# Moving the norms, the logits and the choice of expert groups within the steps of a graph-attention and mixture-of-experts kernel

## The reference

```python
def layernorm(x): return (x - mean(x)) / sqrt(var(x) + 1e-5)
# graph attention
h = layernorm(x) @ W.T + b_W
e = (h @ a1)[:, None] + (h @ a2)[None, :] + b_a
e = where(e > 0, e, 0.2 * e)
x = x + softmax(where(adj > 0, e, -9e15), axis=1) @ h
# experts
xf = layernorm(x)
logits = xf @ Wr + br                       # 64 experts
gates = softmax(top_k(logits, 2))
x = x + sum over the two experts of gate * (relu(xf @ W1[e] + b1[e]) @ W2[e] + b2[e])
```

## Time and profile before

| what | value |
|---|---|
| median of 3 runs | 276.71 us (275.14 to 277.4) |
| profiled execution | 275.16 us, of which the span of the profile is 273.4 |
| granted PE clock, mean | 0.926 |
| PE / DVE / ACT / POOL busy | 227.0 / 208.4 / 180.2 / 167.0 us |
| start of DVE's step 8, 9 | 60.81, 74.11 |
| start of DVE's step 12, 13 | 90.90, 103.39 |
| start of DVE's step 14, 15 | 109.07, 120.67 |
| evac(15) of ACT starts | 135.32 |

### The profile page before, as it was taken

How to read it: one execution, slowest core, us unless ns; L and a number is a source line. 1 busy time by engine, 2 the same in 40 slices (tenths; PEclk the granted TensorE clock), 3 DMA queues, 4 the chain that set the end, 5 groups by cost and what they waited for, 6 DMA issues and landing times.

```text
span 273.4 us, 6241 instructions
## 1 busy us (share of the span) xinstructions
PE 227.0 (83%) x1863; PEld 215.0 (79%) x1863; DVE 208.4 (76%) x587; ACT 180.2 (66%) x425; POOL 167.0 (61%) x212
## 2 busy tenths in 40 slices
PE   1494899999699966978884749999999999999840
PEld 1354899999689966978773639999999999999740
DVE  6879999996999799699455505889886766676465
ACT  2748989999298947758334336887877777777300
POOL 5770003450899889778577753455888888866500
PEclk9999799999799999799995557999999999999995
DMA  6988665589429817108931122222168701100067
GB/s 155 210 161 152 129 119 79 159 228 236 120 66 284 229 39 272 41 10 320 418 120 39 51 63 66 71 66 63 46 185 295 246 31 38 35 31 22 31 198 273
DMA packets 11120, 36.89 MB, mean 135 GB/s; under 512 B 2256, under 2 KB 2832, under 8 KB 10320
## 3 DMA queue, kind: packets, MB, share of 16 engines
q0 software_dynamic: 5232, 14.98, 24.1%
q1 hardware_dynamic: 5424, 21.11, 22.6%
q10 hardware_dynamic: 432, 0.40, 0.7%
HBM read 39.36 MB, written 5.51 MB: 164 GB/s over the span
## 4 chain that ended last, share of the span: by engine, by line
PE 60%; DVE 15%; POOL 7%; DMA 7%; issue 5%; ACT 3%; SPq 1%; POOLq 0%; DVEq 0%; ACTq 0%
PE bank L1146 17%; PE bank L1158 16%; PE bank L1039 12%; PE bank L1015 8%; DVE arena L753 5%; POOL table L431 5%; DMA xs<-in_x 2%; DMA arena<-result 2%; PE bank L980 2%; PE bank L1135 2%; PE bank L1058 1%; PE bank L1055 1%; DMA rows_in<-table,arena 1%; DVE idx L773 1%; DVE hot L779 1%
## 5 line engine op out<-in xcount | busy, mean ns | idle before, releaser
L1039 PE MATMUL bank<-arena 128*128 128x130 f32 x512 | 61.5, 276 | 0.0
L1146 PE MATMUL bank<-arena 128*128 x384 | 60.9, 283 | 0.1
L1039 PEld LDWEIGHTS bank<-arena 128*128 128x128 f32 x512 | 59.5, 192 | 0.5 <-ACT arena L576 0.3
L1158 PE MATMUL bank<-w2s,arena 128*128 x384 | 59.2, 277 | 0.2 <-issue 0.2
L431 POOL DMA_INDIRECT table<-rows_in,pos x32 | 48.7, 1522 | 8.9 <-issue 8.5
L1146 PEld LDWEIGHTS bank<-arena 128*128 128x128 f32 x384 | 52.0, 197 | 0.6 <-issue 0.3
L1158 PEld LDWEIGHTS bank<-w2s,arena 128*128 128x128 f32 x384 | 51.0, 193 | 0.6 <-issue 0.6
L907 DVE SCALAR_TENSOR_TENSOR arena<-bank,arena 128x128 f32 x96 | 33.6, 350 | 22.3 <-PE bank L1158 21.0
L654 ACT ACTIVATE arena<-bank,arena 128x128 f32<-128x128 f32 x96 | 35.1, 366 | 19.0 <-PE bank L1146 17.7
L1015 PE MATMUL bank<-ident,arena 128*128 128x128 f32 x256 | 35.5, 299 | 12.9 <-DVE arena L753 12.9
L576 ACT ACTIVATE arena<-bank 128x512 f32<-128x512 f32 x64 | 34.0, 597 | 14.9 <-PE bank L1015 14.6
(11 more groups left out here) (195 smaller groups left out, 282.1 us busy)
## 6 DMA issues: line engine op xcount, KB each, us to landing
arena<-in_adj POOLq DMA_DIRECT2D x16, 512.0 KB, 6.6
w2s<-in_w SPq DMA_DIRECT2D x8, 768.0 KB, 4.5
arena<-in_w SPq DMA_DIRECT2D x6, 1024.0 KB, 9.3
arena<-in_w SPq DMA_DIRECT2D x4, 512.0 KB, 4.7
w2s<-in_w SPq DMA_DIRECT2D x4, 512.0 KB, 3.9
xs<-in_x SPq DMA_DIRECT2D x4, 256.0 KB, 6.5
arena<-result SPq DMA_DIRECT2D x2, 512.0 KB, 4.4
arena<-result SPq DMA_DIRECT2D x4, 256.0 KB, 5.9
```

The source lines that it names most:

```text
L1039: ins = pe.matmul(OB[t % 2][:, 0:D + 2], pt_r[:, t % 2, j, :], h[:, j, :], start=(j == 0), stop=(j == T - 1))
L1146: ins = pe.matmul(hp(p, b), w1u[:, p % UW, P * b:P * b + P], xT_all[:, bass.ds(column, P)], start=True, stop=True)
L1158: ins = pe.matmul(yp(p), hT[:, p % UH, b, :], w2s[:, bass.ds(u, 1), b, :].rearrange("p e d -> p (e d)"), start=(b == 0), stop=(b == HB - 1))
```

## The change

Groups 0 to 3 are early now. Norms of tiles s-4 and s-3 stand at the end of every even ACT step, behind `evac(s-1)`. PE transposes a group in the middle of `attend(LAST+2)`, ahead of its ninth product, makes the logits behind the products of that step, and counts behind `attend(LAST+3)`. ACT copies into `x2T` in step LAST+4 ahead of the evac. DVE chooses (`top2`) in step LAST+4 behind leaky, for groups 0 to 2; `place` stays in step LAST+5 behind leaky. On POOL the scatters of tiles 8 and 9 leave step 15: one tile's stand ahead of `rstd_of(6)`, the other's between it and `rstd_of(7)`.

```diff
-    PLACED = [(0, 0, 9), ..., (1, 7, 15), (2, 8, 15), (2, 9, 15)]
-    EARLY = 3
-    NORMED = [(5 + 2 * i, 2 * i) for i in range(5)]
+    PLACED = [(0, 0, 9), ..., (1, 7, 15)]
+    EARLY = 4
@@ POOL, behind the loop
+            place(2, 8)
             rstd_of(6)
+            place(2, 9)
             rstd_of(7)
@@ ACT
             def evac(t):
                 for b in range(4):
-                    for q in range(NG):
-                        if b == 2 and q < EARLY and t == LAST[q] + 3:
-                            route_a(q)
...
                 if s >= 3:
                     deviation(s - 3)
-                for at, t in NORMED:
-                    if s == at:
-                        norm(t)
-                        norm(t + 1)
                 for q in range(EARLY):
-                    if s == LAST[q] + 5:
-                        route_b(q)
-                if s == T - 1:
-                    route_a(3)
+                    if s == LAST[q] + 4:
+                        route_a(q)
                 if s >= 1:
                     evac(s - 1)
-                if s == T - 2:
-                    norm(T - 6)
-                    norm(T - 5)
+                if s >= 4 and s % 2 == 0:
+                    norm(s - 4)
+                    norm(s - 3)
+                for q in range(EARLY - 1):
+                    if s == LAST[q] + 4:
+                        route_b(q)
@@ DVE
                     residual(s - 3)
-                for q in range(EARLY):
-                    if s == LAST[q] + 5:
+                leaky(s - 1)
+                for q in range(EARLY - 1):
+                    if s == LAST[q] + 4:
                         top2(q)
-                leaky(s - 1)
-                for q in range(EARLY):
                     if s == LAST[q] + 5:
                         place(q)
@@ PE, attend(t)
-                for q in range(EARLY):
-                    if t == LAST[q] + 3:
-                        route_a(q)
-                if t == T - 2:
-                    route_b(3)
...
                     for q in range(EARLY):
-                        if j == T // 4 and t == LAST[q] + 3:
-                            route_b(q)
+                        if j == 8 and t == LAST[q] + 2:
+                            route_a(q)
...
                 ins.then_inc(s_o, 1)
+                for q in range(EARLY):
+                    if t == LAST[q] + 2:
+                        route_b(q)
@@ PE, the loop
-                for q in range(EARLY):
-                    if s == LAST[q] + 4:
-                        route_c(q)
                 turn(s)
                 attend(s)
-                if s == T - 3:
-                    route_a(3)
-                if s == T - 2:
-                    route_c(3)
+                for q in range(EARLY):
+                    if s == LAST[q] + 3:
+                        route_c(q)
```

More of the change, by code:

```diff
@@ L25, in build @@
     LAST = [START[q + 1] - 1 for q in range(NG)]
-    PLACED = [(0, 0, 9), (0, 1, 10), (0, 2, 11), (0, 3, 11), (1, 4, 13), (1, 5, 13), (1, 6, 13), (1, 7, 15), (2, 8, 15), (2, 9, 15)]
-    EARLY = 3
-    NORMED = [(5 + 2 * i, 2 * i) for i in range(5)]
+    PLACED = [(0, 0, 9), (0, 1, 10), (0, 2, 11), (0, 3, 11), (1, 4, 13), (1, 5, 13), (1, 6, 13), (1, 7, 15)]
+    EARLY = 4
     LNS = [(t, t + 2) for t in range(0, T - 2, 2)] + [(T - 2, T - 1), (T - 1, T)]
```

## The result

The changed kernel is slower: 288.38 us median of 4 runs (285.05 to 290.48) against 275.92 of the kernel before, ratio 1.045 (95% interval 1.029 to 1.061). Measured once more beside the experiments (e10), it came to 289.6, ratio 1.049 (1.042 to 1.055). Medians are over all executions of a kernel, while the ratios leave out those in a slower state, here the 290.48 and in e1 the 289.4. The profiled execution took 288.86 us, its span is 287.1, 13.7 us more than before. The profile before was of an execution of 275.16 us.

What follows compares the result with a forecast made beforehand. DVE was taken to set the pace of ordinary steps, ACT close behind. Terms +5.8, +4.8, -1.3, -1.6 and +0.5 gave +8.2 on 275.16, so 283.4, stated as 284.0 us; range 278 to 289.

Steps and rivals of the forecast that it cites:

- my own sum: Whole kernel: the terms for groups and tail add +8.2 us, forecast 284.0, own range 281 to 286.5, chance 0.60.
- the rival of the slower clock: PE behind its longer holes: lower clock adds +5.0 us over three groups, 288.4; chance 0.15.
- Group 0, +5.8: Loop up to DVE's step 9: norms waiting for POOL make logits late, step 9 starts at 79.9 against 74.11.
- The chain caught by leaky: POOL's chain for tiles 2 and 3: ends at 60.3 untouched, 62.9 if held by leaky; 62.8 taken.
- Group 1, +4.8: DVE's steps 9 to 13: POOL's late scale holds norms some 3 us; step 13 starts at 113.95, +4.8 more.
- Group 2, -1.3: DVE's steps 13 to 15: two-tile group with norms in time gains 1.3 us; step 15 starts at 129.95.
- The condition: Four-tile groups on DVE: break even only if logits (L') come 3.30 us sooner, since the next step's work follows top2.
- Tail, -1.6 and +0.5: After DVE's step 15 starts (D_15): evac(15) gains 1.6 us with ACT's r15 at +2.35; group 4's transposes cost 0.5.
- The sign that I named: Tail: ACT's 4.7 us wait for POOL gone, as one sign that the forecast is right.
- No wait for POOL, 276.6: Norms on ACT never wait for POOL, only their 0.98 us counts: +1.4 us, 276.6; chance 0.12.
- Scatters pass leaky: POOL's scatters run unheld beside leaky, so group 1 loses less: +5.2 us, 280.4; chance 0.08.
- Faster: ACT has caught up, so L560 of step l+4 (l: group's last tile) starts with DVE's scores: -3.3, 271.9; chance 0.05.

Runs made afterwards that it cites:

- e10: Changed kernel as it is, measured once more against the kernel before; 289.6 us, ratio 1.049.
- e1: Changed kernel with DVE's top2 back in step LAST+5 ahead of leaky, all else as changed; 285.6 us, ratio 1.037 to the kernel before.
- e6: Changed kernel with top2 back in step LAST+5 ahead of leaky and norms as plain copies not waiting for POOL; 270.92 us, ratio 0.985 to the kernel before.
- e2: Changed kernel with norm a plain copy that does not wait for POOL, scale and shift left out; 277.16 us, ratio 1.008 to the kernel before.
- E9: Changed kernel with unused extra transposes on PE ahead of its wait for norms in groups 0, 1 and 3; 286.19 us, ratio 1.039 to the kernel before.
- e8: Kernel before with ACT's norms alone moved to the end of even steps; 283.82 us, ratio 1.031.

## Why the prediction was right, and where its sum was short

I forecast 284.0 in a range of 278 to 289, slower with chance 0.85; it took 288.38, slower. The direction and the mechanism in the loop were right. The size was 4.4 us short, outside the 281 to 286.5 that I gave my own sum; only the room left for other cases holds it, and the second measurement, 289.6, lies above the range. That 288.38 is the figure of the rival of the slower clock is luck: the excess is of POOL and the clock together. Step by step:

- **Group 0, +5.8.** Measured +5.0 in the two profiles, +5.3 counted from step 0. ACT's first wait was 1.55 (1.6 forecast), L560's counterpart in step 7 came at 63.06 (63.8), the max at 68.39 (69.3). The chain caught by leaky is the term that I chose between bounds: 62.8, and it ended at 62.03. The nearest row, a chain caught in its first operation, was 0.8 us too dear; here two short operations slipped through and only the third was held. (The 1.44 that I gave an untouched chain was the wrong reading: it is how far the caught one ended behind leaky. Untouched it took 1.61, from 76.80 to 78.41. The sum goes by the caught one.) How close this is to chance the second profile of the same kernel, e10, shows, in step 4:
```profile
47.54 2.35 DVE L748 SCALAR_TENSOR_TENSOR arena<-arena,tneg 128x2048 f32<-128x2048 f32 x1
47.59 2.88 POOL L413 TENSOR_TENSOR rstd<-ve,expo 128x2 f32<-128x2 f32 x1
...
52.18 1.09 ACT L587 ACTIVATE rows_in<-xs,nm,rstd 128x256 f32<-128x256 f32 x2 [3.06 <-POOL nm L415]
...
81.72 2.28 DVE L742 CUSTOM_DVE_ANT_0 arena<-arena 128x2048 f32<-128x2048 bf16 x1
```
POOL's third operation began 0.05 us behind leaky here and was held, where in the first profile it began 0.25 ahead of it (46.89, 0.72 us long). ACT waited 3.06, not 1.55, and step 9 came 61.72 us behind step 0, not 58.79. The two executions took 291.67 and 288.86 us: group 0's loss is 5 us in one and 8 in the other.
- **Group 1, +4.8.** Measured +4.7 (33.95 against 29.28 us from step 9 to 13). But ACT waited 1.40 where I had 3: its own evac(9) had become late, behind a turn(8) of 3.10 us, so that the late scale and the slow clock lay side by side. The sum was right because the scale alone set it: L415 ended at D_9 + 16.9, as forecast.
- **Group 2, -1.3.** Measured -1.5.
- **The condition** (L' must come 3.3 us sooner) held: e1 shows 7.5 us from max to step 9 in the old order, the changed kernel 10.7, and e6 against e2 gives 6.2 us for the order in two such groups.
- **Tail, -1.6 and +0.5.** This is the step that failed. Evac(15) came 19.6 us behind the start of step 15, where I had 13.0 and before had 14.65: +4.9, not -1.6. I took r15 as D_15 + 2.35, that is, I let the norms of tiles 10 and 11 end in time. They ended 3.75 late, POOL's chain being held by scores and then by leaky behind scatters that had run to 128.18. The other 2.9 us are PE at its lower level, in the second half of attend(13) (3.67 us, not 1.96), the logits and turn(14); attend(14) took 3.75, the upper level's time. E9 bears this out: with the clock up the same distance was 16.64. The +0.5 behind evac(15) was right: spans differ by 13.7, evac(15) by 13.1. The sign that I named, ACT's wait for POOL in the tail gone, was half wrong: the one ahead of evac(15) fell from 4.73 to 1.58, and the new one of 3.75 stands ahead of step 15.
- **The rivals.** No wait for POOL, 276.6: e2 made that case, with norms 0.35 us a pair cheaper, and took 277.16. Slower clock, 288.4: I priced it as three turns on the path; where it can be counted it is about 3 us, in group 3, the place that I had named as without cover. Scatters pass leaky: they do not, L430 at 125.14 began as leaky ran (125.00) and took 3.04 us, as in the kernel before. Faster: nothing of it was seen in groups 0 and 1; step 7 of ACT came at 63.06, not below 58.

What stays open: in the tail POOL and clock are told apart by rows and by e9, but the wait for POOL also makes the holes behind which the clock falls, so that their shares of the whole loss can't be added up cleanly. Nor is it shown how much of e8's excess is the clock, nor why POOL's chain starts some tenths later in one execution than in another.

## What to carry to other kernels

When a small operation is moved earlier on an engine with an in-order queue, look up when its input is ready, and not only when its consumer wants it: norm pairs put ahead of 5 us of ScalarE's work let a chain of four tiny GpSimd operations set when the logits came. When a choice is moved from the middle of a step to its end, the work that used to cover the wait now stands behind it; the new input must come earlier by that work, or the move loses. And a part of a losing change can be a gain by itself: test the parts alone.

## What the runs showed of the hardware

GpSimd's tiny operations (128 x 2 values) took 0.18 to 0.74 us (two of over 200 about 1.0) where VectorE ran none of its 2048-wide operations of two inputs. Begun beside one of those, they ended with it or up to 0.65 us behind it, and so took up to 2.88 us; over all profiles of this case the only ones that escaped had begun within 0.05 us of its start, as L411 at 58.84 in the changed kernel, 0.03 us behind leaky and 0.19 long. I had counted leaky as the only holder; VectorE's scores (L742) holds them too (2.86 us at 128.81, begun 0.01 behind it), and a one-input operation begun beside leaky took 2.35 (e1, 59.42). That agrees with the Trainium skill, "SBUF — State Buffer", section "Who interferes with whom", by which an operation of VectorE with two SBUF inputs contends with GpSimd instructions that read SBUF. The same section infers that descriptor generation needs the write side, by which leaky would let scatters through. Here it did not: a scatter begun beside leaky took 3.04 us, an unheld one 0.96. A scatter also reads its row numbers from SBUF (`pos`), so the first rule may be what holds it; no run here tells the two apart.

The other thing not expected is that useless transposes in a hole of PE pay: 3.44 us of them kept the granted clock at 1.00 where it had been 0.53, and made the kernel 1% faster. The 12 in the hole of group 0 did not keep it up: 0.57 in 68 to 72 us with and without them.
